# A four-layer graph network: where the edge multiplicities are counted, and when they are scattered

## The reference

```python
x = x + L0(relu(ln(x)))   # attention: per edge, logits from feat_all[type, src] and [type, dst],
                          # softmax over the edges of one destination, then
                          # h = segment_sum(alpha[..., None] * feat_src_e, dst)
x = x + L1(relu(ln(x)))   # GCN: segment_sum(h[src] * norm, dst), softmax over 10 clusters
x = x + L2(relu(ln(x)))   # segment_sum(x[src] + relu(ea @ ee_w1 + ee_b1) @ ee_w2 + ee_b2, dst), MLP
x = x + L3(relu(ln(x)))   # segment_sum(h[src], dst) / degree, two linear maps
```

## Time and profile before

| | us |
|---|---|
| median of 3 runs (3606.77 to 3622.25) | 3610.38 |
| profiled execution, its own time | 3592.67 |
| its span, first to last instruction | 3590.8 |
| PE, DVE, ACT, POOL busy | 2931.4, 1831.5, 1347.6, 1002.6 |
| mean granted TensorE clock, share of full speed | 0.894 |

### The profile page before, as it was taken

The page is one execution under the profiler, slowest core; times in us unless marked ns, Lnnn a source line. Parts: engine busy times, 40 slices in busy tenths (PEclk is TensorE's granted clock), DMA queues, the critical chain, the costliest instruction groups (busy, mean ns, idle before and its releaser), DMA issues.

```text
span 3590.8 us, 48300 instructions
## 1 busy us (share of the span) xinstructions
PE 2931.4 (82%) x14984; PEld 1914.3 (53%) x14984; DVE 1831.5 (51%) x5022; ACT 1347.6 (38%) x4115; POOL 1002.6 (28%) x1048
## 2 busy tenths in 40 slices
PE   2677776299999989840488789988999999999998
PEld 2433332288888888830473344444555555545545
DVE  6455555177777777620374344334555555542334
ACT  1233333377677777720352040003444444420000
POOL 2255445656566666677200000000000000000000
PEclk6688888599999999965677789999999999999999
DMA  8844443333333333310016533331000000022232
GB/s 257 343 131 145 140 139 119 95 88 88 83 89 87 90 84 87 90 30 2 8 49 228 170 114 103 101 118 39 6 6 4 4 6 6 15 69 83 76 101 81
DMA packets 245034, 320.91 MB, mean 89 GB/s; under 512 B 121467, under 2 KB 162084, under 8 KB 240740
## 3 DMA queue, kind: packets, MB, share of 16 engines
q1 hardware_dynamic: 191412, 182.34, 17.9%
q0 software_dynamic: 49104, 104.11, 9.9%
q10 hardware_dynamic: 4320, 31.95, 2.2%
HBM read 240.69 MB, written 77.59 MB: 89 GB/s over the span
## 4 chain that ended last, share of the span: by engine, by line
PE 52%; DVE 13%; issue 10%; another core or an unknown queue 9%; ACT 6%; DMA 4%; DVEq 3%; SPq 2%; ACTq 0%
PE PS L1173 15%; PE PS L1018 13%; PE PS L984 6%; PE PS L959 5%; PE PS L997 4%; PE PS L842 3%; DMA BG<-a_d 3%; ACT BG L673 2%; DVE BG L1724 2%; DVEq L1603 2%; SPq L341 2%; DMA key_d<-SUMS 1%; DVE OHB L1451 1%; ACT SL L756 1%
## 5 line engine op out<-in xcount | busy, mean ns | idle before, releaser
L1588 DVE TENSOR_TENSOR SUMS<-SUMS,PS 128x640 f32 x500 | 409.1, 818 | 426.5 <-remote 193.5
L534 POOL DMA_INDIRECT BG<-feat_d,IDXST x500 | 484.5, 969 | 316.2 <-PE PS L959 163.0
L525 POOL DMA_INDIRECT a_d<-VAL,IDXS x499 | 483.0, 968 | 318.2 <-DVE VAL L1445 157.1
L1173 PE MATMUL PS<-BG,SL 128*128 128x512 f32 (+1 forms) x1440 | 538.1, 529 | 12.2 <-ACT SL L756 12.2
L673 ACT ACTIVATE BG<-BG,SL 128x64 f32<-128x64 f32 x2000 | 513.5, 337 | 0.0
L565 POOL MEMSET BG<- 128x7680 f32 x1 | 6.5, 6501 | 1451.8 <-DVE MV L1855 1451.8
L1173 PEld LDWEIGHTS PS<-BG,SL 128*128 128x128 f32 x1440 | 276.2, 194 | 251.6 <-issue 222.4
L984 PE MATMUL PS<-W1A,X 65*128 65x256 f32 x1000 | 279.8, 403 | 102.3 <-issue 90.8
L959 PE MATMUL PS<-OHB,BG 128*128 128x128 f32 x2000 | 339.2, 293 | 0.5 <-issue 0.5
L997 PE MATMUL PS<-OHB,X 128*128 128x128 f32 x2000 | 319.6, 283 | 22.3 <-issue 21.8
L997 PEld LDWEIGHTS PS<-OHB,X 128*128 128x128 f32 x2000 | 290.0, 197 | 36.1 <-issue 22.0
(11 more groups left out here) (301 smaller groups left out, 4181.3 us busy)
## 6 DMA issues: line engine op xcount, KB each, us to landing
BG<-a_d SPq DMA_DIRECT2D x171, 256.0 KB, 4.2
AL<-a_d SPq DMA_DIRECT2D x137, 256.0 KB, 2.6
a_d<-BG POOLq DMA_DIRECT2D x30, 1088.0 KB, 40.4
feat_d<-SUMS ACTq DMA_DIRECT2D x30, 1040.0 KB
BG<-rel_d SPq DMA_DIRECT2D x100, 160.0 KB
SL<-key_d SPq DMA_DIRECT2D x50, 320.0 KB
X<-in_edge_attr_dram SPq DMA_DIRECT2D x124, 128.0 KB
SUMS<-a_d SPq DMA_DIRECT2D x52, 256.0 KB, 2.6
```

What stands on the lines that cost most here:

```text
L525: pool.indirect_dma_start(a_d.rearrange("n (w o) -> (n w) o", o=1), bass.IndirectOffsetOnAxis(ap=IDXS[:, t:t + 1], axis=0), VAL[:, t:t + 1 ...
L534: pool.indirect_dma_start(RING[:, t // NB % 3, t % NB, :], None, feat_d.rearrange("n (r d) -> (n r) d", r=R), bass.IndirectOffsetOnAxis(ap ...
L1173: last = pe.matmul(PS[:, to + q, 0:width], lhs[:, i, c, :], w[:, c, q * width:(q + 1) * width], start=(c == 0), stop=(c == kc - 1))
L1588: add = tt(a, a, SUM_AT[n % 3].rearrange("p (a n) -> p a n", a=5), ALU.add)
```

## The change

The prologue counts CT = 3 tiles a round, all on VectorE; ScalarE's `counts`, its buffer and the wait of VectorE for it go. So 150 tiles are scattered in the prologue in place of 250. The loop counts at all 20 tiles of a batch (CB = 20), 350 tiles in all, which ends at tile 349. From gather 86 on a scatter follows every second gather, 207 in all. The last 142 scatters come after gather 499, and now each waits for `agg_ps`: scatter i of them until 442 + i tiles are summed, at most 500.

```diff
-        CT = 5
+        CT = 3
         SOON = CT * IT
-        CB = 13
+        CB = 20
@@ gpsimd
-                if t >= LEAD and (t - LEAD) % 4 == 0:
+                if t >= LEAD and (t - LEAD + 1) * 1 // 2 > (t - LEAD) * 1 // 2:
                     scatter_late(counted)
                     counted += 1
-            for n in range(counted, TR):
+            for i, n in enumerate(range(counted, TR)):
+                pool.wait_ge(s("agg_ps"), 20 + min(T - 3 * NB + 2 + i, T))
                 scatter_late(n)
@@ scalar
-            def counts(u):
-                act.wait_ge(s(f"rows{u % 2}_in1"), 32 * (u // 2 + 1))
-                for k in range(CA):
-                    last = act.activation(DIFF[:, k, :], KEYR[:, u % 2, k, :], ACT.Abs, scale=-1.0,
-                                          bias=KEY0[:, CT * u + k:CT * u + k + 1])
...
-                    while counted < IT and 4 * NT * (counted - 1) <= (4 * t + q) * IT:
-                        counts(counted)
-                        counted += 1
@@ vector
-                for k in range(CA, CT):
+                for k in range(CT):
...
-                dve.wait_ge(s("act_counts"), u + 1)
                 cp(VAL[:, v], MULT0[:, v]).then_inc(s("val_ready"), 1)
```

More of the change, by code:

```diff
@@ L237, in gnn @@
         SAME0 = SLF[:, 2 * CT * P:5 * CT * P // 2].bitcast(BF16).rearrange("p (k n) -> p k n", k=CT)
-        CA = 3
-        DIFF = SA[:, 5688:5688 + CA * P].rearrange("p (k n) -> p k n", k=CA)
         IDENTB = IOTA[:, 0:P // 2].bitcast(BF16)
@@ L589, in _ @@
             act.activation(B1C, B1C, ACT.Relu).then_inc(s("b1_relu"), 1)
-            def counts(u):
-                if u:
-                    act.wait_ge(s("act_counts"), u)
-                act.wait_ge(s(f"rows{u % 2}_in1"), 32 * (u // 2 + 1))
-                for k in range(CA):
-                    last = act.activation(DIFF[:, k, :], KEYR[:, u % 2, k, :], ACT.Abs, scale=-1.0,
-                                          bias=KEY0[:, CT * u + k:CT * u + k + 1])
[L599 to L604, removed]
             act.wait_ge(s("elr_done"), 2 * 4)
-            counted = 0
             for t in range(NT):
```

## The result

| | before | changed |
|---|---|---|
| median | 3609.64 us (3606.77 to 3622.25, 4 runs) | 3496.99 us (3492.02 to 3500.61, 4 runs) |
| span of the profiled execution | 3590.8 us | 3494.0 us |
| mean granted clock | 0.894 | 0.904 |

The ratio is 0.968 (95% interval 0.9655 to 0.9706): 113 us faster by the medians, 97 by the two profiled executions, against -79 predicted. In some of the experiments the kernel before takes 415 us less, and there the same change makes the kernel slower; that comes behind.

What follows compares the result with a forecast made beforehand. The prediction took GpSimd's back-to-back indirect DMAs, which hold TensorE's signals, to set the pace of the first half. Terms -133 + 124 - 188 + 118 = -79 us gave 3513.7, with 17.7 for the median 3531; range 3435 to 3650.

Steps and rivals of the forecast that it cites:

- (a): Prologue: three scatters a round end VectorE's waits for held signals; rounds of 6.5 us instead of 9.4, -133 us.
- (b): First 60 gathers and first 26 tiles: same gathers back to back in the same order, 0 us.
- (d): Last 60 tiles: 58 scatters go one per summed tile with pauses, 102 us instead of 290, -188 us.
- (e): Behind the loop: 84 scatters back to back nearly stop home, 187 us instead of 69, +118 us.
- (c): Loop of 413 gathers: more scatters lengthen GpSimd's bursts, 2.23 us a tile instead of 1.93, +124 us.
- bound of two tiles a release: Slow end for the loop: only two tiles pass per release of signals, 2.37 us a tile, +182 us.
- R4: Rival: home gets on beside the 84 scatters behind the loop, +39 there, -158 in all, 3452 us; chance 0.12.
- 18 us of silence: Behind the loop: signals return 18 us after GpSimd's last issue, before most of home follows.
- R1: Rival, slower: the loop's bursts run together, 2.6 us a tile, +277 in the loop, 3684 us; chance 0.14.
- R3: Rival: prologue bursts of three still held or TensorE's clock low, rounds of 8 us, -64, 3600 us; chance 0.12.
- R2: Rival: the loop is slowed less, 2.0 us a tile, +29 there, -174 in all, 3436 us; chance 0.18.
- R5: Rival: VectorE's counts stretch GpSimd's issues, +34 us in the loop, 3565 us; chance 0.04.

Runs made afterwards that it cites:

- e11: Changed kernel without the waits on `agg_ps`, plus one small gather behind the last scatter: 3600.42 us against 3616.41 for the kernel before, ratio 0.9955.
- e10: Changed kernel with a short GpSimd fill ahead of gathers 20 to 59 and the last 83 scatters: 3495.6 us against 3614.48 for the kernel before, ratio 0.9672.
- e12: Changed kernel with rounds of four, one scatter to three gathers, fills before 45 scatters, small last gather: 3421.53 us against 3616.41 for the kernel before, ratio 0.9453.
- e3: Changed kernel with one scatter to four gathers in the loop instead of one to two: 3349.86 us, ratio 1.0482 to the kernel before.
- e1: Kernel before with only the waits on `agg_ps` added to the scatters behind the last gather: 3219.19 us against 3194.96, ratio 1.0073.
- e5: Changed kernel itself, run again without edit: 3267.02 us against 3192.99 for the kernel before, ratio 1.0225.
- e6: Kernel before, without edit, profiled on the same chip as the changed kernel's rerun: 3189.28 us in one execution.

## Why the prediction was right, and where not

**The direction** came from the cause it named: while GpSimd issues indirect DMAs 1.26 us apart, signals are late, and what it issues with what pauses sets the pace. e11 shows it for the last 60 tiles and home, e10 for home, both on held chips; that signals alone are what is late, it doesn't bear out (above, home). But the prediction took it for a property of the kernel on its chip. It depends on something outside the kernel as well, and on a free chip the same change is 2.2% slower. No row of the first profile shows it, so that the forecast met a held chip was luck.

**The number** is in part luck as well. (a) and (b) gained 22 us more than forecast, (d) 2 and (e) 31 more, and (c) lost 38 more; together the sum is 18 us off. The 17.7 us added for the median are off too: the profiled execution of the changed kernel lies 1 us under its median, that of the kernel before 17 to 18.

**(a)** Forecast 6.5 us a round, measured 292/46 = 6.35; the waits of the earlier trace rows are gone. TensorE's clock was granted at 0.98 there instead of 0.85, so its work took 264 us and not the 277 that I feared as the next bound. That the shorter row of scatters freed the rounds, and not the missing hand-over to ScalarE, is argued from the earlier trace rows and not shown: no held run changed one alone. In e12, held, with four scatters a round and no hand-over, VectorE waited 18.6 us in three waits.

**(b)** Forecast 0, measured -11 in the windows. From the first gather to gather 86 it is 137.1 us before and 134.2 now, -3. The rest is a misread window: the one from 606 doesn't begin with the gathers, but with the last round of five scatters, which belongs to (a). So the prologue gained 152 us and not 140.

**(c)** The mis-sized term: 2.23 us a tile forecast, 959/413 = 2.32 measured, 38 us more. The cycles of four and five were right (5.98 and 7.40 read, 6.08 and 7.50 found). Wrong was that bursts have only four or five issues, in equal numbers, with three tiles in each. The commonest burst of the changed kernel has two gathers and a scatter and takes 4.64 us, 2.32 us a tile; bursts of five, 2.50 a tile, outnumber those of four, 2.03 a tile; those of six take 2.27. The bound of two tiles a release, 2.37, was the nearer end.

**(d)** Forecast -188, measured -190.5, and e11 shows that it is the waits' doing: 285 us without them.

**(e)** Forecast +118, measured +87, R4 at +39. The step that failed is "in an endless burst it nearly stops", carried over from the loop to home. Home did 18 of its 30 node tiles in the row of scatters: ten by 1680, eight of them at full pace, then eight more at 7 to 14 us each. The 18 us of silence were 13 (VectorE's next tile is at 1776.47). So 51 us and not 81 were left behind the row (1763.5 to 1814.5).

**The claim that VectorE's and ScalarE's signals are prompt** held in the prologue and the loop and fails in home, where L1610 waits for VectorE's own.

**The rivals.** R1 (2.6 us a tile) and R3 (rounds of 8 us) did not occur. A pace near R2's, 1.93 us, is what a free chip gives, and there it is a loss, since the kernel before has 1.74. R4, home beside the scatters, came in part: home went on, but slowly. R5: the issues have 976 ns in the median instead of 960, 16 ns on a scatter; e3, with the same counts on VectorE and half the scatters in the loop, has 959, so it isn't the counts that lengthen them. The warning of the Trainium skill (SBUF — State Buffer, section "SBUF: two separate sides"), that VectorE may lock GpSimd out, shows in none of these medians.

## What to carry over

Before tuning against idle time whose cause is a late signal, look whether it is there on every chip: here a difference of 415 us came and went between groups of runs, and a change that gains 3.2% with it loses 2.2% without it. In a row of GpSimd's indirect DMAs count issues times 1.27 us as the floor, leave pauses where others need its signals or their own, and put DMAs that nobody reads soon where GpSimd is idle. If the waits of such an edit can be had alone, try them alone: here they were nearly the whole gain of the changed kernel on a held chip (e11), and in the kernel before a loss of 24 us on a free one (e1).

## What the runs showed of the hardware

- The same kernel before took 3193 to 3195 us in the median of some groups of runs and 3599 to 3616 in others, and the runs of one group lie within 1% of each other. Chip 6 came up with both kinds, so it is no fixed property of that chip; what sets it stays open.
- Where signals are held, signals come late while GpSimd issues indirect DMAs 1.26 us apart, gathers and scatters alike (the first addition 85 us behind the first gather instead of 43 in e5; the last 60 tiles 285 us in e11 instead of 99.5). 1.46 to 1.56 us apart with a fill between them, the scatters don't hold home (e10, 1.56 us a node tile).
- In a long row, on a held chip, signals of VectorE to itself are late too, by 5.8 us at 1709.96, and instructions that wait for nothing start 0.7 to 1.4 us apart (1686.13 to 1693.13). It takes some 15 us of the row until that begins (1657.41 to 1673).
- The last scatter signals 18.1 us after its issue on a free chip (e6) and 18.2 to 19.4 on held ones (e10, e12), also at the wider distance and with a gather behind it. The Trainium skill, DMA: Bandwidth & Descriptors, section "Anatomy of one DMA — SWDGE (gpsimd) path", gives about 2.0 us for the fixed part; by it, an estimate, the first adjacency load of e6 would start 16 us earlier. The trace disagrees for this last one, and the rows decide.
